# Retention layer and mixture of experts on 8 cores: the transposes for the expert input are emitted one tile later, into another PSUM bank

## What is computed

```python
x = x + _layernorm(_L0_attn_ref(_layernorm(x, axis=-1), ...), axis=-1)
x = x + _layernorm(_L0_ffn_ref(_layernorm(x, axis=-1), ...), axis=-1)
...
    retention = jnp.einsum('bhsd,bhtd->bhst', q, k) / math.sqrt(Dh)
    retention = retention * decay_matrix[None]
    out = jnp.einsum('bhst,bhtd->bhsd', retention, v)
    g = jax.nn.silu(x @ wg.T)
    return out * g @ wo.T
```

## Time and profile before

| what | us |
|---|---|
| median of the timed runs (3) | 4477.41 |
| lowest | 4475.08 |
| the profiled execution, its own time | 4471.33 |
| its longest span (core 7, whose rows are shown) | 4469.6 |
| spans of the other seven cores | 4455.7 to 4469.1 |
| own stage on core 7, tiles 0 to 15 | about 1263 to 2618 |

### The profile page before, as it was taken

How to read it: one execution, slowest core, us unless ns; L and a number is a source line. 1 busy time by engine, 2 the same in 40 slices (tenths; PEclk the granted TensorE clock), 3 DMA queues, 4 the chain that set the end, 5 groups by cost and what they waited for, 6 DMA issues and landing times.

```text
span 4468.5 us, 37046 instructions; the slowest of 8 cores (4455.7 to 4469.6 us)
## 1 busy us (share of the span) xinstructions
PE 2730.2 (61%) x12862; PEld 1252.2 (28%) x13084; DVE 1633.8 (37%) x3649; ACT 447.4 (10%) x662; POOL 94.8 (2%) x120
## 2 busy tenths in 40 slices
PE   0035555555544444443444424999999979999996
PEld 0012222222222222221222212444344334444442
DVE  0035555656543333333333343222222332222224
ACT  0000000000000111101011011110101110101101
POOL 0000000000000000000000000000000000000000
PEclk9996767777776666766766756999999989999998
DMA  9410000010000000000000005363543642633632
GB/s 119 82 44 24 29 29 29 24 33 24 29 0 19 10 10 19 10 10 19 10 10 17 7 5 88 49 95 49 84 66 48 123 96 41 100 60 54 95 54 74
DMA packets 155193, 199.53 MB, mean 45 GB/s; under 512 B 46690, under 2 KB 120434, under 8 KB 154690
## 3 DMA queue, kind: packets, MB, share of 16 engines
q0 software_dynamic: 94384, 123.81, 18.8%
q1 hardware_dynamic: 60626, 73.36, 5.6%
HBM read 293.65 MB, written 27.30 MB: 72 GB/s over the span
## 4 chain that ended last, share of the span: by engine, by line
PE 53%; DVE 26%; issue 9%; DMA 6%; ACT 3%; SPq 2%; DVEq 1%; another core or an unknown queue 0%; ACTq 0%; POOL 0%; POOLq 0%
PE pB L377 8%; PE pA L377 7%; PE pS L924 6%; PE pB L924 3%; PE pA L924 3%; PE pKT L924 3%; PE pT L924 3%; PE pT L974 3%; PE pO L924 3%; PE pQT L924 3%; PE pO L974 3%; PE pKT L974 3%; PE pQT L974 2%; DVE R_all L431 2%; SPq L296 2%
## 5 line engine op out<-in xcount | busy, mean ns | idle before, releaser
L377 PE MATMUL pB<-wkT,xlnfm 128*128 128x512 bf16 x510 | 269.0, 528 | 191.5 <-DVE xlnfm L367 189.5
L377 PE MATMUL pA<-wkT,xlnfm 128*128 128x512 bf16 x454 | 240.1, 529 | 87.4 <-DVE q_tm L406 68.7
L948 DVE TENSOR_TENSOR hcm<-h1s,cb_bf 128x1024 bf16<-128x1024 bf16 x128 | 88.6, 692 | 559.6 <-PE pS L924 339.4
L924 PE MATMUL pA<-Xln_fm,wr 128*128 128x512 bf16 x550 | 229.4, 417 | 81.4 <-DVE cb_bf L908 81.4
L924 PE MATMUL pS<-Xln_fm,wr 128*128 128x512 bf16 x1128 | 258.6, 379 | 2.1 <-DMA wr<-We 0.9
L924 PE MATMUL pB<-Xln_fm,wr 128*128 128x512 bf16 x576 | 239.1, 415 | 18.7 <-DMA wr<-We 12.0
L974 PE MATMUL pO<-wr,h 128*128 128x512 bf16 x554 | 215.8, 389 | 21.3 <-DVE xres L1020 21.1
L974 PE MATMUL pT<-wr,h 128*128 128x512 bf16 x576 | 224.2, 389 | 1.5 <-issue 0.4
L974 PE MATMUL pKT<-wr,h 128*128 128x512 bf16 x576 | 223.6, 388 | 1.4 <-issue 0.2
L974 PE MATMUL pQT<-wr,h 128*128 128x512 bf16 x552 | 214.5, 389 | 14.9 <-DVE xres L1020 14.9
L924 PE MATMUL pKT<-Xln_fm,wr 128*128 128x512 bf16 x576 | 218.3, 379 | 1.2
(11 more groups left out here) (209 smaller groups left out, 4092.0 us busy)
## 6 DMA issues: line engine op xcount, KB each, us to landing
wr<-We POOLq DMA_DIRECT2D x96, 1024.0 KB, 14.2
xtile<-x_pre SPq DMA_DIRECT2D x48, 512.0 KB, 3.7
wr<-ws POOLq DMA_DIRECT2D x12, 1024.0 KB, 14.7
xtile<-x_own SPq DMA_DIRECT2D x16, 512.0 KB, 3.6
xscr<-xtile SPq DMA_DIRECT2D x16, 512.0 KB, 2.6
xres<-xscr SPq DMA_DIRECT2D x16, 512.0 KB, 3.3
out<-xres SPq DMA_DIRECT2D x16, 512.0 KB, 2.6
wq_bf<-wq POOLq DMA_DIRECT2D x1, 2048.0 KB, 25.0
```

The source lines that it names most:

```text
L377: return eng.matmul(pb[:, :], xf_ap[:, ch * 128:(ch + 1) * 128], wT[wname][:, ch, half * 512:(half + 1) * 512], start=(ch == 0), stop=(ch ...
L924: return eng.matmul(pb[:, :], wsrc[:, s1, ch, ich * 128:(ich + 1) * 128], Xln2_fm[:, ch, tok0 + th * 512:tok0 + (th + 1) * 512], start=(ch ...
L948: return eng.tensor_tensor(hcm[:, :], h1s[:, :], cb_bf[:, :], ALU.mult)
```

## The change

The x2T step of tile t is no longer at the end of `own_B(t)`. It is emitted by `emit_xln2_T(t)` inside `own_B(t + 1)`, behind the evictions `qfm` and `kfm` and ahead of `qs_bf`, and it uses bank `pQT` instead of `pT`. For the last tile it is emitted after the loop. The same number of instructions of each kind is left. (`emit_xln2_T` was there before, but nothing called it.)

```diff
     def emit_xln2_T(t):
         transpose8(ks_bf[:, :], "ks_bf",
                    Xln2_fm[:, :, t * 128:(t + 1) * 128],
-                   f"Xln2_{t}", f"o{t}x2T")
+                   f"Xln2_{t}", f"o{t}x2T", pbank=pQT, pres="bank_pQT")
...
+        if t > 0:
+            emit_xln2_T(t - 1)
+
         def qsf(eng):
             return eng.tensor_tensor(qs_bf[:, :, :], qfm[:, :, :], gbcast_sb[:, :, :], ALU.mult)
...
         ln_apply(ks_bf[:, :], "ks_bf", xa, xr, rstd3, nmr3, rres3, f"o{t}l3")
-        transpose8(ks_bf[:, :], "ks_bf",
-                   Xln2_fm[:, :, t * 128:(t + 1) * 128],
-                   f"Xln2_{t}", f"o{t}x2T")
...
                 own_B(t, st)
                 st = stn
+            emit_xln2_T(nt_run - 1)
```

## The result

The changed kernel takes 4514.1 us (median of 10; lowest 4504.5) against 4476.9 us of the kernel before in the same runs (lowest 4472.5). The ratio is 1.0078, with a 95% interval of 1.0065 to 1.0091: 35 us slower. The forecast was 4491 us, with a range to 4508; the loss is about two and a half times the 14 us that I expected. The forecast held a difference under 2% for one that can't be told from no change; the interval here is 0.13% to either side, so this loss is clear. Some executions were disturbed on one die; the ratios leave them out, and where I compare experiments I give the lowest time of each, for that reason.

The account below looks back on a forecast made before the run. The own stage was taken as bound by one chain of waits, PE and DVE taking turns. 4471.3 us + 18.9 - 5.2 = 4485.0; with the median 6.1 us above the profiled execution, about 4491 us, range 4472 to 4508.

Parts of the forecast that it names:

- What bounds the stage: Own stage, change of tiles: the path of spill, load and statistics sets when `xlnfm` starts; x2T ends earlier.
- Nothing taken away in 14 changes of tiles: In 14 of 15 changes of tiles, moving x2T's eight transposes and copy away is worth nothing.
- rival 1: x2T was on the path in every tile: 15 x 5.2 = 78 us gained, less 19, 4418 us; chance 3%.
- The wait of 1.22 us for bank `pT`: At the change of tiles, next input's transposes wait for x2T's eviction; 18 us by the rule on banks, nothing by the row.
- Tile 15, minus 5.2: At the change to tile 15, with no further load, `xlnfm` starts 0.11 us after L350: 5.2 us gained, once.
- Plus 1.07 or 1.42 us in the middle: Tiles 1 to 15: x2T between `kfm` and `qs_bf` delays `qs_bf` by 1.07 (higher clock) or 1.42 us (lower).
- The shares: Of tiles 1 to 15, 7 pay the higher-clock price of 1.07 us and 8 the lower-clock 1.42: 18.9 us.
- the sum itself: Whole kernel: 4471.3 us + 18.9 - 5.2 = 4485.0, with an expected median of about 4491 us.
- a sign of being wrong: A shrinking tile period, or a share of matmuls at the lower clock changing by more than a few a tile.
- rival 4: Unbroken PE idle stretch keeps projections q, k, v longer at the lower clock: 2.9 us x 15, 4534 us; chance 9%.

Follow-up runs that it names:

- e9: Kernel before with `own_A(t + 1)` moved behind the rotary embedding of k, x2T left at the end of the tile; lowest 4372.4 us.
- e10: Changed kernel with `own_A(t + 1)` moved behind the rotary embedding of k; lowest 4329.6 us, ratio 0.9706 to the kernel before.
- e4: Changed kernel with x2T of the tile before placed behind the rotary embedding of q instead of ahead of `qs_bf`; median 4470.5 us, ratio 0.9989.
- e2: Kernel before with two DVE operations, result unused, added ahead of `qs_bf`; ratio 1.0085, lowest 4506.2 us.
- e5: Changed kernel with eight further PE transposes of `ks_bf` into `pT` behind the third layer norm, result unused; ratio 1.0097, lowest 4513.1 us.
- e1: Kernel before with one DVE operation, result unused, added ahead of `qs_bf`; ratio 1.0009, lowest 4473.2 us.
- e3: Kernel before with four DVE operations, result unused, added ahead of `qs_bf`; ratio 1.0126, lowest 4524.9 us.
- e7: Changed kernel with x2T emitted behind `qs_bf` instead of ahead of it; ratio 1.0028, lowest 4479.7 us.
- e8: Changed kernel with x2T behind the rotary embedding of q and `own_A(t + 1)` behind that of k; 4283.5 us, ratio 0.9562 to the kernel before.

## Why the prediction was wrong

- **What bounds the stage: right.** Spill, load and statistics held `xlnfm`, with x2T hidden beside them. In the changed kernel `xlnfm` still starts 0.11 us behind the statistics, and e9 and e10 show the reverse: once the load is out of the way, the same edit gains.
- **Nothing taken away in 14 changes of tiles: right**, and rival 1 is out. The wait of 1.22 us for bank `pT` did vanish, and nothing came of it, as the row had said.
- **Tile 15, minus 5.2: right at its place** (5.33 to 0.11 us behind L350), **but the gain didn't show** in the tile's length, 78.5 us against 78.4 on seven of eight cores. The delay took 1.4 of it and the clock the rest: on these cores q, k, v and `wo` of tile 15 have 49 to 51 matmuls at the lower clock, against 31 to 35 before, and 18 at 0.21 us are 3.8 us. On core 4, with 33, the tile takes 75.1 us and the gain is there.
- **Plus 1.07 or 1.42 us in the middle: right.** Measured 1.02 and 1.41. The shares were not quite right, since more tiles than 8 of 15 met x2T at the lower clock (12 of 15 on core 1). That is 1.3 us a tile, 20 in all, against 18.9.
- **The step that failed is the sum itself.** It let each tile grow by its delay and kept the number of matmuls at the lower clock as it was. In the changed kernel 6.0 more a tile run there, 1.3 us, 19 us over the stage; that is what the prediction had named as a sign of being wrong. The same clock ate the 5.2 us of tile 15. This is the side of rival 4, to which I gave 9%, at less than half its price of 2.9 us a tile, and that it came true is luck: its reason, the unbroken idle stretch, is not what the runs show. e4 keeps the clock with the idle stretch, e2 loses clock without it, and e5 does not get the tile's length back. What the runs show in its place is when q starts. A delay in the middle of the tile moves that start, and e2, with nothing but 1.4 us of delay, loses clock as well, though less than the change (2.5 matmuls a tile against 6.0, 0.3 us beyond its delay against 1.3).
- **Why a delay costs clock.** The Trainium skill (TensorE: Matmul & The Clock Gate, What's actually happening) says that the monitor behind the clock runs freely of the kernel. The traces agree: on each core all 120 changes of the granted clock between the first and the last `ks_bf`, before and after, lie whole multiples of one step apart, to within 0.004 us, whatever the tiles do. So the engine must wait for a moment it doesn't set, and the higher clock comes 2.6 to 6.0 us after q's start, as the start happens to fall: on core 1 of the changed kernel it comes 4.1 us after it in tile 7 and 5.7 to 6.0 in eight other tiles, against 3.3 in tile 6 before. Of 120 starts of q on eight cores, it comes within 3.6 us in 107 before, 100 in e1, 93 in e3 and e4, 46 in e2 and 20 in the changed kernel. The tile's length follows. From q to q it is 85.4 us in the kernel before where the clock comes within 3.6 us, and 88.2 where it comes more than 5 us after the start; the changed kernel has 86.7 and 89.7, both longer by about its delay.
- **What stays open.** A tile that starts at another moment also ends at another, so the next one meets the clock differently, and how often q starts late doesn't grow in step with the delay: under 3.0 us, 109 of 112 tiles take 88 or 89 us with the same count in q at the lower clock as before, while under 1.3 or 1.4 us they are mixed, up to 90.9. Why the changed kernel starts q late more often than e2, which has the same delay of the mask, is not shown; that its transposes now stand elsewhere among PE's work is a rival that no run tested alone at this delay. The same holds for e7 against e1. There the tiles of like starts are alike (85.5 and 85.4 us for early clocks, 88.5 and 88.4 for late ones), and only the share of late ones differs, 16 of 52 on cores 4 to 7 against 19 of 104.

## What to carry to other kernels

Before a step is moved out of a wait, ask which path ends last at the join, and price the new place by the engine that is in turn there. An in-order queue hides much: the statistics of the tile after next stood ahead of this tile's eviction, and moving those was worth 187 us (e4 to e8) where moving the visible wait cost 35. And where PE works in bursts between waits, the clock is part of the sum: a repeated delay cost from half its own length (e1) to twice it (the change), so count the matmuls at each level in the changed kernel as well.

## What the runs showed that I had not expected

- The cost of a repeated delay is no straight line: 0.6, 1.4 and 3.0 us a tile lengthened it by 0.3, 1.7 and 3.1 us. The changed kernel with 1.4 us more delay grew by only 0.5.
- The cores settle alike: in e9 all eight have tiles of 78.5 us on average, in e10 all have 76.1, though they work independently.
- Eight transposes in a row take 0.61 us at the higher clock and 1.01 at the lower, about the ratio of the score matmuls.
